# A post-norm decoder block on one core: TensorE multiplies a block of weights with itself at five places around the hand-over of the two stages

## The reference

```python
x = _layernorm(x + _L0_attn_ref(x, wq, wk, wv, wo))      # per sequence: q, k, v, rope, causal softmax, out @ wo.T
x = _layernorm(x + _L0_xattn_ref(x, ctx_4096, weight))   # cosine of neighbouring context columns times x,
                                                         # then a convolution with three taps
x = _layernorm(x + _L0_ffn_ref(x, A, B, Wr, br))         # eight experts of rank 16, soft routing
```

## Time and profile before

| quantity | value |
|---|---|
| median of three executions | 1433.07 us (1432.07 to 1433.4) |
| the profiled execution, its own time | 1434.46 us |
| its span, first to last instruction | 1432.6 us |
| TensorE busy | 1368.6 us, 96% of the span |
| VectorE, ScalarE, GpSimd busy | 1091.2, 932.3, 983.9 us |
| mean granted clock of TensorE | 0.98 of full |

### The profile page before, as it was taken

The page is one execution under the profiler, slowest core; times in us unless marked ns, Lnnn a source line. Parts: engine busy times, 40 slices in busy tenths (PEclk is TensorE's granted clock), DMA queues, the critical chain, the costliest instruction groups (busy, mean ns, idle before and its releaser), DMA issues. The chain is left out here.

```text
span 1432.6 us, 32298 instructions
## 1 busy us (share of the span) xinstructions
PE 1368.6 (96%) x8288; PEld 1060.1 (74%) x8288; DVE 1091.2 (76%) x3869; ACT 932.3 (65%) x3258; POOL 983.9 (69%) x936
## 2 busy tenths in 40 slices
PE   6999999999999999999985899999999999999995
PEld 4777777777777777777753688888888888888873
DVE  5677777777777777777775487788887788887774
ACT  5688878788787877878775354555554455554543
POOL 2777777777677776777764666777776777776763
PEclk9999999999999999999996999999999999999997
DMA  7345445454444544445466856655666766766651
GB/s 242 97 126 157 128 135 150 119 157 121 139 152 118 152 123 145 147 121 152 120 193 175 204 150 167 174 148 161 164 156 165 174 150 160 165 153 164 161 118 45
DMA packets 108861, 213.03 MB, mean 149 GB/s; under 512 B 26640, under 2 KB 32272, under 8 KB 108816
## 3 DMA queue, kind: packets, MB, share of 16 engines
q1 hardware_dynamic: 108624, 212.25, 53.9%
q10 hardware_dynamic: 192, 0.26, 0.1%
HBM read 131.83 MB, written 34.47 MB: 116 GB/s over the span
## 5 line engine op out<-in xcount | busy, mean ns | idle before, releaser
L435 PE MATMUL wo_ps<-weights,halves 128*128 128x512 f32 x2304 | 573.8, 400 | 11.8 <-DVE weights L614 11.7
L435 PEld LDWEIGHTS wo_ps<-weights,halves 128*128 128x128 f32 x2304 | 423.9, 190 | 128.6 <-issue 34.6
L697 ACT ACTIVATE pexp<-sm,smin 128x128 f32<-128x128 f32 x1024 | 398.8, 393 | 122.8 <-DVE smin L565 120.9
L1056 PE MATMUL wo_ps<-weights,halves 128*128 128x512 f32 x1488 | 400.9, 402 | 2.6 <-DVE yz L1159 2.6
L827 POOL TENSOR_TENSOR pn<-pexp,prec 128x512 f32<-128x512 f32 x256 | 268.6, 1049 | 146.9 <-DVE prec L572 146.9
L1409 POOL TENSOR_TENSOR prods<-prod,prods 128x512 fp32r<-128x512 f32 x192 | 259.3, 1358 | 134.5 <-ACT prods L1303 129.5
L1056 PEld LDWEIGHTS wo_ps<-weights,halves 128*128 128x128 f32 x1488 | 273.4, 190 | 61.6 <-issue 4.3
L565 DVE CUSTOM_DVE_ANT_0 sm<-s_ps,mask_t 128x128 f32<-128x128 f32 x1024 | 231.7, 281 | 78.7 <-PE s_ps L465 77.5
L1303 ACT CAST prods<-prod 128x512 fp32r<-128x512 f32 x192 | 118.8, 621 | 165.8 <-DVE prod L1193 129.2
L1193 DVE TENSOR_TENSOR prod<-att,x 128x512 f32<-128x512 f32 x192 | 187.0, 989 | 12.2 <-DMA att<-sim_scratch 9.7
L697 ACT ACTIVATION_READ_ACCUMULATOR pexp<-sm,smin 128x1 f32 x1024 | 194.8, 190 | 0.0
(11 more groups left out here) (99 smaller groups left out, 1661.2 us busy)
## 6 DMA issues: line engine op xcount, KB each, us to landing
att<-sim_scratch SPq DMA_DIRECT2D x192, 252.0 KB
pt<-blocks SPq DMA_DIRECT2D x636, 64.0 KB, 2.0
ctx_t<-in_ctx SPq DMA_DIRECT2D x32, 576.0 KB, 4.6
raw<-in_xT SPq DMA_DIRECT2D x32, 512.0 KB, 3.8
raw<-ot_scratch SPq DMA_DIRECT2D x32, 512.0 KB, 6.7
xn<-in_x SPq DMA_DIRECT2D x32, 512.0 KB, 7.4
out<-late SPq DMA_DIRECT2D x32, 512.0 KB, 6.2
ot_scratch<-ot SPq DMA_DIRECT2D x63, 256.0 KB, 2.1
```

Of the source, the lines that this page charges most:

```text
L435: mm = pe.matmul(qkv_ps[(par + g) % 2][:], xs[:, par, xl, k], w_sb[:, wl, g, k], start=(k == 0 and n == 0), stop=(k == KT - 1 and n == 2))
L697: ins = nc.scalar.activation(pexp[:, c % 2, i * P:(i + 1) * P], sm[:, c % 2, i * P:(i + 1) * P], ACT.Exp, bias=smin[:, c % 2, i:i + 1], sc ...
L1056: mm = pe.matmul(wo_ps[n][:], os_t[:, par, ol, k], wo_sb[:, wl, k, n * BANK:(n + 1) * BANK], start=(k == 0 and m == 0), stop=(k == KT - 1 ...
```

## The change

A function `keep_running` issues so many matmuls of the first 128 columns of `wo_sb` with its first 512 columns, into a bank that nobody reads. It is called at five places, all on TensorE:

- part 1, step 32, slot 13: a wait for `qt_in` at 64 (the count for sequence 31), 14 matmuls into `turn_ps`, then `score(31, 1)`;
- part 1, step 33, slots 9 and 17: 20 matmuls into `turn_ps` ahead of each `weigh(31, ...)`;
- part 2, step 1: 10 matmuls into `ffn_ps[0]` ahead of slot 0;
- part 2, step 1, slot 11: 18 matmuls into `ffn_ps[0]` ahead of the first unit of the convolution.

```diff
+def keep_running(pe, bank, wo_sb, products):
+
+    for _ in range(products):
+        pe.matmul(bank[:], wo_sb[:, 0, 0, 0:P], wo_sb[:, 0, 0, 0:BANK], start=True, stop=True)
...
             for s in range(SLOTS):
+                if at_step(t, B) and s == 1 + NJ * PERIOD:
+                    pe.wait_ge(qt_in, NU * B)
+                    keep_running(pe, turn_ps, wo_sb, 14)
+                if at_step(t, LAST) and s in (9, 17):
+                    keep_running(pe, turn_ps, wo_sb, 20)
                 if valid(a):
                     if s % (NJ * PERIOD) == 1:
                         score(a, 1 - par, s // (NJ * PERIOD))
...
             o, c, f, z = t, t - 1, t - 2, t - 3
+            if at_step(t, 1):
+                keep_running(pe, ffn_ps[0], wo_sb, 10)
             for s in range(SLOTS2):
+                if at_step(c, 0) and s == conv_at(c)[0]:
+                    keep_running(pe, ffn_ps[0], wo_sb, 18)
```

## The result

The changed kernel takes 1438.22 us (median of six executions, 1436.51 to 1440.65), against 1431.68 us (1428.01 to 1433.4) for the kernel before in the same comparison. The ratio is 1.0050, with a 95% interval of 1.0033 to 1.0067: slower, by 4.7 to 9.6 us. The profiled execution took 1436.74 us, with a span of 1434.9.

The account below looks back on a forecast made before the run. A chain of waits was taken to bound the hand-over, and TensorE to bound from 817.45 us on. Terms + 4.3 + 0.1 - 0.3 = + 4.1 us on the median 1433.07 gave 1437.2 us, range 1435.3 to 1440.0.

Parts of the forecast that it names:

- The chain at the hand-over: Between parts 1 and 2: waits from the copy of q through the second score to part 2 decide its start.
- The first filler, + 4.3: Ahead of step 32's second score: 5.2 us of matmuls less 0.9 saved by the score, all reaching the hand-over.
- no row from 756.82 on leaves it more than a few tenths of slack: From VectorE's mask to part 2: a delayed score passes on, with at most a few tenths of a us absorbed.
- The second and third filler, + 0.1: Step 33, ahead of both products with v: second hidden, third about 0.1 us, with 0 and 2.1 as ends.
- The rival that they run at the low clock: Later fillers, with 2.1 us more at step 33: low clock makes the kernel slower, 1439.2 us; chance 0.17.
- The fourth and fifth, - 0.3: Start of part 2 to first convolution: fillers hidden, full clock there gains 0.3 us (0 to 0.4).
- A miss of the clock here costs up to 3 us on TensorE: Part 2 before VectorE's sum at 805.00: low clock costs up to 3 us, with equal room, counted as nothing.
- theory D: Follow-up theory on part 2: its loss is only a longer load of x in one profile, 10.41 us against 9.55.
- The size of the gain there: First convolution in part 2: full clock removes VectorE's 0.37 us wait at 805.00, and more doesn't come.
- The signs of being wrong: Copy at 773.04 not moving, part 2 under 3 us later, or its stretch to the last GpSimd wait over 1 us shorter.
- the second loss: Follow-up theory on part 2: early TensorE idles, clock falls, leading work starts at 1.2 GHz; +1.5 to +2.5 us.
- The rival by which TensorE decides at the hand-over: From the second filler on, TensorE's work leads: 7.0 us back against 4.3 lost, 1430.4 us; chance 0.05.

Follow-up runs that it names:

- the second one's 1.0030: The unchanged changed kernel measured again with more runs against the kernel before: ratio 1.0044 (1.0030 to 1.0058), 12 executions.
- with the gaps filled: Whole change plus 4 matmuls ahead of part 2's step 2 and 6 ahead of the convolution's fourth unit, against the kernel before: 1.0033; without the first filler: 1.0010.
- the one that kept the clock full to 812 us: Changed kernel without the first filler, plus 4 and 6 matmuls where TensorE waits in part 2, against the kernel before: ratio 1.0010 (0.9997 to 1.0022).
- first filler and part 2: Changed kernel without the two fillers of step 33, so first, fourth and fifth stay, against the kernel before: ratio 1.0036 (1.0024 to 1.0048).
- first filler behind the score: Changed kernel with the 14 matmuls behind step 32's second score instead of ahead, other fillers kept, against the kernel before: ratio 1.0003 (0.9991 to 1.0015).

## Why the prediction was right, and where it was not

1437.2 us was predicted, with 1435.3 to 1440.0 as the range; 1438.22 was measured. The direction, and the place and mechanism of the main term, held. The ratio is 1.0050 against 1.0029 worked out, which lies just outside the first interval and just below the second one's 1.0030. So the size was forecast too small, 4.1 us against 6.5. That the time itself came out within 1.0 us is in part luck: the kernel before measured 1431.68 in this comparison and not the 1433.07 that the sum starts from, and the first filler's term was too large at the hand-over while the term of part 2 had the wrong sign.

- *The chain at the hand-over* (copy of q, second score, VectorE, SyncE, in_wb, ScalarE, part 2): shown. Moving the same 14 matmuls from ahead of the score to behind it took the loss away (1.0044 to 1.0003 on one chip), and 14 more at the same place moved the start of part 2 by 3.6 us.
- *The first filler, + 4.3*: at the mask it was 4.1, 5.08 us of filler (5.2 worked out) less the 0.9 that the score gets back; the filler took 5.02 to 6.06 us in the seven profiles with 14 matmuls. At the start of part 2 it was 3.4 in the mean of the profiles. The step "no row from 756.82 on leaves it more than a few tenths of slack" was wrong about SyncE. The ten moves took 6.22 to 7.21 us to issue in the six profiles without the first filler, 6.9 on average, and 6.21 to 6.24 in all eight with it. So 0.6 us of the delay is taken back in the queue. Why an issue is sometimes held up there was not tried.
- *The second and third filler, + 0.1*: shown as nothing, 1.0001. The rival that they run at the low clock did not occur: all 20 took 4.69 to 4.85 us in every profile that has them.
- *The fourth and fifth, - 0.3*: the step that failed. "A miss of the clock here costs up to 3 us on TensorE, with as much room until VectorE needs the sum at 805.00; I put it at nothing." I followed the clock to the first convolution and stopped there. VectorE's wait of 0.37 us did go, but TensorE, being early, then waited for GpSimd twice, and the clock fell just where its work leads to the end. From VectorE's addition of x on, that is + 1.1 and + 1.2 us in the changed kernel's two profiles instead of - 0.3. That the low clock there is the cause is shown by the levels of the table: with the gaps filled, by 10 matmuls more and nothing less, 18.14 and 18.21 became 16.19. The rest of the longer stretch, 1.07 and 0.77 us, is x that landed later, as in theory D; where the first filler is left out and the gaps are not filled, that is all of it.
- *The size of the gain there* was too small as well. I took VectorE's 0.37 us for all that an earlier full clock could give. The kernels with 3.4 us of low clock instead of 6.8, and without fillers in part 2, are 0.9 us shorter from the addition on (16.15 to 16.18 against 17.05). How 0.37 becomes 0.9 was not tried; VectorE's product behind its wait took 1.52 us in the kernel before and 0.70 in the one with the fillers of step 33 only.
- *The signs of being wrong.* Wrong "if part 2 starts less than 3 us later": counted from T0 it was 2.2 in the first pair of profiles, and 3.4 in the mean. That sign is met by the pair and not by the mean; in the pair, 1.0 us is the copy of the queries that came early.
- *What stays open.* Why, with the gaps not filled, the clock was low for 6.8 us in the three profiles with the first filler and for 3.4 in the three without it: whether that is more than chance three runs each can't tell. In time, the second loss was not resolved. Without the first filler the ratios of 0.9997, 0.9999 and 1.0003 agree with the profiles, which have no loss from the addition on (- 0.1 us). With it, 1.1 us is 0.08%, which the intervals of 1.0036 with part 2's fillers and 1.0036 without can't show. The sum of the means, 3.4 at the hand-over, 0.5 to the addition and 1.1 behind it, is 5.0 us, 0.35%: inside the intervals of the changed kernel (1.0033 to 1.0067, 1.0030 to 1.0058), but at their lower ends.
- *The rival by which TensorE decides at the hand-over* (1430.4): fallen. With the clock full at the products with v and at the first convolutions, nothing came back in time. The Trainium skill's TensorE: Matmul & The Clock Gate, in HAM oscillation — how this bites in real kernels, counts the penalty as the throttled time times one half. By that rule the 13.9 us in which TensorE was busy in the last two low stretches of the earlier trace rows would be worth 7.0 us (an estimate). The runs do not agree: without the first filler they measured 0 (0.9999, 0.9997, 1.0001), and so did the one that kept the clock full to 812 us (1.0010, with 1 inside its interval).

No kernel here beat the one before. The best of them, the fillers of part 2 alone, is at 0.9997, which can't be told from it.

## What to carry to other kernels

A filler has to stand ahead of the wait that it is to fill, and needs an output that is free before that wait ends; if its own operand or bank waits for the same event, it only delays what stands behind it. Ask at each low stretch of the clock whether the work in it is on the chain. And where a filler does make the engine faster, follow it to the next wait: an engine that is early stands idle there, and may start the work that counts at the low clock. Before a stretch of two profiles is compared, split it at the point where a DMA lands: here 1.07 us of a later x looked like a loss of TensorE's.

## What the runs showed of the hardware

- The clock can fall while TensorE is at work. In the changed kernel it was full when the first filler began at 751.34, behind 4.76 us of idle time, fell at 751.8 and rose at 755.2, with TensorE busy throughout.
- How long work has to wait for the full clock differs between runs of one pattern: 3.7 us from the restart at 801.27 in the kernel without the first filler, 6.0 us from the restart at 807.22 in the changed one.
- The clock fell behind two gaps of 1.07 and 1.58 us that were 1 us apart in the changed kernel, and behind two such gaps (0.97 to 1.33 and 1.56 to 1.59 us) in all six profiles that have them. With 4 and 6 matmuls in them (1.08 and 1.52 us) it stayed up in both kernels. Behind one gap of 1.53 us at 804.3, in the kernel with the first three fillers, it did not fall.
- Ten issues of the same moves on SyncE took between 6.21 us (first filler and part 2) and 7.21 us (first filler behind the score).
